# One operand in PSUM for small VectorE instructions of a spectral GNN kernel, and the refinement's products at other units

## The chip, the cores and the metric

The kernel runs on one core of one Trainium2 chip. The metric is the device time of one launch in microseconds (us), from the first to the last instruction with what lies around it; lower is better. TensorE is called PE in the profile, VectorE DVE, ScalarE ACT, GpSimd POOL, SyncE SP.

## What is computed

Two layers on 64 graphs of 256 nodes with 256 features, f32 throughout. Layer 0 is three graph convolutions (256 to 512 to 1024 to 256 features) with the weights `adj * adj`. Layer 1 needs the eigenvectors of a 256 x 256 symmetric matrix made of `adj`, which all graphs share.

```python
# layer 0
h = jnp.maximum(_layernorm(x, axis=-1), 0.0)
h = relu(slconv(h, adj, adj, W1)); h = relu(slconv(h, adj, adj, W2))
x = x + slconv(h, adj, adj, W3)          # slconv: (adj * adj) @ (h @ W)
# layer 1
h = jnp.maximum(_layernorm(x, axis=-1), 0.0)
_, U = jnp.linalg.eigh(L_norm)           # L_norm: scaled Laplacian of adj
agg = jnp.einsum('mn,bnd->bmd', U.T, h)
out = jnp.maximum(agg @ W1 + b1, 0.0) @ W2 + b2
x = x + jnp.einsum('nm,bmd->bnd', U, out)
```

## The kernel before

The graphs go in pairs: 32 pairs, 0 to 31. One pair of layer 0 is a fixed list of 40 units of matmuls on PE (`plan`): 4 `hid` (units 0 to 3), 4 `agg2` (4 to 7), 14 `P` units (8 to 21, two each of P1, P5, P6, P3, P7, P2, P4, seven products in place of eight), 2 `agg` (22, 23, the first product of the next pair), 14 `G` units (24 to 37, another seven products) and 2 `res`. The last pair has no `agg`, so its G units begin at 22. A unit writes one of four PSUM banks in turn; ACT copies each result to SBUF (`evacuate`, L756), POOL forms the sums between products (L556, L564, L572 to L590, all 128 x 512 or 128 x 256 f32 in SBUF), and ACT applies the ReLU to six of them (`finish`, L762). G1 waits for all six (`fin`, L1515).

Beside the pairs runs the eigenvalue problem, mostly one chain on DVE:

- **Householder steps** k = 0 to 253, over pairs 0 to 20. For k up to 126 the vectors span two blocks of 128 (`householder_two`, L945), after that one (`householder_one`). PE lays a column of two numbers per partition out as a row with transposes (L1455): first `col` (`step_x`), then `qcol` (`step_q`). Between these two, and behind the second, PE works off the slice of the pair's units that a table (`GROUPS`: 11 steps per pair in pairs 0 to 7, 12 in 8 to 10, then 13, 12, 14 and 13) gives to the step. DVE scales q by a scalar (L997) before it uses the row of q (L1000), updates A (L963, L967) and makes the next `col` (L1009). POOL keeps each reflector (L503, L504) as soon as v is there (L988), and then does what sums are due.
- **Sturm counts**, four times (`sturm_counts`, L1123): 256 small dependent instructions per direction and, every 16 pivots, a block of start values (L1140) and a block of sign counts (L1167). The first count ends in a product on PE at unit 34 of pair 22 (`COUNTS_AT`).
- **Eigenvectors of the tridiagonal matrix** (L1237 to L1282): two chains of factors, a second pass over all of them (L1249 to L1259), the twist index, two scans each way, a norm whose root ACT takes (L853).
- **Refinement** in pairs 30 and 31: PE turns Z (L1678), then twice Gram and T Z (L1685, L1686), Z^T(TZ) (L1690) and the correction (L1694, L1695), with DVE work between; then the signs, another turn and the products U and U^T (L1699, L1700). `REFINE_AT`, `TURN_AT` and `VECTORS_AT` say before which unit each is placed, counted from unit 0 of pair 30 (40 and more is pair 31).

Layer 1 follows for all pairs (from 2055 us). Engines run their own instruction lists in order, and wait for one another through semaphores only. In `householder_two` every DVE instruction but L997 has at most one tensor operand in SBUF and the other, if any, in PSUM, or is one element wide; L997 reads `qcol` and writes `qn`, both two elements per partition in SBUF.

## Time and profile before

| | us |
|---|---|
| median of 3 runs | 2314.66 |
| range of the runs | 2314.52 to 2315.05 |
| the profiled execution | 2315.77 |
| its span, first to last instruction | 2314.0 |
| Householder steps on two blocks | 19 to 777 |
| Householder steps on one block | 777 to 1380 |
| pairs 21 to 29 beside Sturm counts and factors | 1381 to 1921 |
| pairs 30 and 31 with the refinement | 1921 to 2055 |
| layer 1 | 2055 to 2314 |
| busy: PE, DVE, ACT, POOL | 2259.6, 2005.7, 1149.3, 1172.5 |

The profiled execution lies 1.1 us above the median, and 1.8 us of it lie outside the span. Two engines are busy nearly all the time, so the busy shares alone don't say which one sets the pace; that is read from who waits for whom in each stage.

### The profile page before, as it was taken

Reading aid. Unit: us, or ns where it says so; the run is one execution under the profiler, and the core shown is the slowest. Engines: PE = TensorE matmul, PEld = TensorE weight load, DVE = VectorE, ACT = ScalarE, POOL = GpSimd, SP = SyncE. Lnnn points to the kernel's source line nnn. Section 1 sums busy time; section 2 is a strip of 40 time slices with the busy share of each in tenths; the row PEclk is TensorE's granted clock in tenths of the full one; section 3 lists DMA queues with packets and bytes.
Section 4 is the critical chain, followed back from the end, with each engine's and each line's share of the span. In section 5 each row is a group of like instructions: output and inputs, shape, how many; then the busy total and the mean of one; then the engine's idle time right before and its main releaser. Section 6 shows DMA issues by size and latency. Waiting matters only on the chain.

```text
span 2314.0 us, 47926 instructions
## 1 busy us (share of the span) xinstructions
PE 2259.6 (98%) x12586; PEld 1898.6 (82%) x12586; DVE 2005.7 (87%) x10807; ACT 1149.3 (50%) x2901; POOL 1172.5 (51%) x1889
## 2 busy tenths in 40 slices
PE   7999999999999999999999999999999999999999
PEld 5777777877787788887777788888888888899998
DVE  7999999999999988888888889999999995447776
ACT  5455555555555555554444444454444444345554
POOL 6445554444555555555554567545555554353332
PEclk9999999999999999999999999999999999999999
DMA  3000000000000000000000000000000001024443
GB/s 103 28 28 10 28 28 27 21 28 28 28 10 28 28 29 28 28 28 28 19 28 28 28 29 19 28 19 28 28 28 28 28 28 37 19 67 130 134 133 107
DMA packets 90033, 90.16 MB, mean 39 GB/s; under 512 B 5376, under 2 KB 89088, under 8 KB 89856
## 3 DMA queue, kind: packets, MB, share of 16 engines
q1 hardware_dynamic: 89856, 88.23, 12.0%
q8 instruction: 58, 0.95, 0.2%
q14 instruction: 119, 0.97, 0.1%
HBM read 54.66 MB, written 33.55 MB: 38 GB/s over the span
## 4 chain that ended last, share of the span: by engine, by line
PE 69%; DVE 24%; ACT 4%; issue 2%; POOL 1%; DVEq 0%; POOLq 0%; ACTq 0%
PE ps L1533 53%; PE ps L1723 10%; DVE A L963 3%; DVE qn L997 2%; DVE A L967 2%; PE ps L1455 2%; ACT squares L711 2%; DVE xrow_sb L972 2%; ACT root_s L713 2%; DVE prods L1000 2%; DVE sc L981 1%; DVE ps L1015 1%; PE ps L1733 1%; DVE sc L984 1%; DVE qcol L986 1%
## 5 line engine op out<-in xcount | busy, mean ns | idle before, releaser
L503 POOL COPY Eb<-sc 128x1 f32<-128x1 f32 (+1 forms) x254 | 47.1, 186 | 525.4 <-DVE v L988 292.3
L1533 PE MATMUL ps<-agg2T,w 128*128 128x256 f32 x1024 | 239.8, 379 | 0.0
L1533 PE MATMUL ps<-hid2T,xin 128*128 128x256 f32 x1024 | 236.2, 379 | 1.6 <-ACT h2T L756 1.6
L1533 PE MATMUL ps<-weightT,hid 128*128 128x256 f32 x1024 | 236.6, 380 | 0.0
L1533 PE MATMUL ps<-w,aggT 128*128 128x512 f32 x512 | 231.4, 593 | 0.0
L1533 PEld LDWEIGHTS ps<-weightT,hid 128*128 128x128 f32 x1024 | 189.3, 191 | 35.4 <-issue 13.0
L1533 PEld LDWEIGHTS ps<-hid2T,xin 128*128 128x128 f32 x1024 | 189.5, 190 | 26.3 <-ACT h2T L756 1.9
L1533 PEld LDWEIGHTS ps<-agg2T,w 128*128 128x128 f32 x1024 | 189.2, 191 | 24.2
L756 ACT ACTIVATE hid2T<-ps 128x512 f32<-128x512 f32 x256 | 151.1, 590 | 95.9 <-PE ps L1533 93.2
L1164 DVE SCALAR_TENSOR_TENSOR ahead<-ps,ne,ahead 128x14 f32<-128x14 f32 (+1 forms) x1024 | 190.2, 228 | 0.0
L1161 DVE RECIPROCAL ps<-ahead 128x14 f32<-128x14 f32 (+1 forms) x1024 | 187.8, 229 | 0.1
L1533 PEld LDWEIGHTS ps<-w,aggT 128*128 128x128 f32 x512 | 92.2, 190 | 90.5 <-issue 89.6
L556 POOL TENSOR_TENSOR hid2T<-agg2T 128x512 f32<-128x512 f32 x64 | 82.0, 1281 | 111.7 <-ACT agg2T L756 111.7
L756 ACT ACTIVATE g<-ps 128x128 f32<-128x128 f32 x256 | 70.2, 276 | 136.8 <-PE ps L1533 136.0
L756 ACT ACTIVATE hid<-ps 128x512 f32<-128x512 f32 x128 | 76.3, 596 | 111.4 <-PE ps L1533 110.9
L756 ACT ACTIVATE agg2T<-ps 128x512 f32<-128x512 f32 x128 | 76.2, 595 | 103.5 <-PE ps L1533 103.2
L762 ACT ACTIVATE hid2T<-hid2T 128x512 f32<-128x512 f32 x192 | 119.1, 620 | 9.6 <-POOL hid2T L564 9.3
L1533 PE MATMUL ps<-w3sum,hid 128*128 128x128 f32 x1024 | 123.8, 275 | 0.0
L1533 PE MATMUL ps<-w,hid2T 128*128 128x128 f32 x1024 | 122.9, 275 | 0.0
L1533 PEld LDWEIGHTS ps<-w,hid2T 128*128 128x128 f32 x1024 | 120.7, 192 | 1.3
L713 ACT ACTIVATE root_s<-root_s,tiny 128x1 f32<-128x1 f32 x254 | 74.8, 295 | 93.7 <-DVE prods L1040 88.5
L1455 PE MATMUL ps<-ident,col 128*128 128x128 f32 x381 | 88.3, 286 | 32.5 <-DVE col L1009 30.4
(386 smaller groups left out, 6326.7 us busy)
## 6 DMA issues: line engine op xcount, KB each, us to landing
xl<-in_x_dram SPq DMA_DIRECT2D x64, 256.0 KB, 2.8
xr<-in_x_dram SPq DMA_DIRECT2D x64, 256.0 KB, 2.9
x_dram<-xr SPq DMA_DIRECT2D x64, 256.0 KB, 2.3
xin<-x_dram SPq DMA_DIRECT2D x64, 256.0 KB, 2.8
out_dram<-xin SPq DMA_DIRECT2D x64, 256.0 KB, 2.2
w<-in_L_gnn_W_dram SPq DMA_DIRECT2D x1, 2048.0 KB, 10.3
...
```

Source lines behind the costliest of these rows:

```text
L503: pool.tensor_copy(Eb[:, bass.ds(k, 1)], sc[:, 4:5])
L556: pool.tensor_tensor(moving_sum(n), a, b, ALU.subtract).then_inc(turn_s, 1)
L711: act.activation(squares[:, c0:N], xr[:, c0:N], ACT.Square, accum_out=root_s[:, 0:1]).then_inc(sq, 1)
L713: act.activation(root_s[:, 1:2], root_s[:, 0:1], ACT.Sqrt, bias=tiny[:, 0:1]).then_inc(root, 1)
L756: act.activation(dst, bank, ACT.Relu if stage in ("hid", "P4") else ACT.Copy).then_inc(evac, 1)
L762: act.activation(block_, block_, ACT.Relu).then_inc(fin, 1)
L963: return dve.scalar_tensor_tensor(A[:, b, rest], p_q[:, rest], vh[:, b:b + 1], A[:, b, rest], ALU.mult, ALU.subtract)
L1161: inverse_made[d] = at(dve.reciprocal(inverse[:, d, :], here[:, d, :]))
L1164: pivot_made[d] = at(dve.scalar_tensor_tensor(there[:, d, :], inverse[:, d, :], ne2[:, off:off + 1], there[:, d, :], ALU.mult, ALU.add))
L1455: ins = pe.transpose(dst[:, P * b:P * b + P], col(b).to_broadcast([P, P]), ident[:, 0, 0:P])
L1533: ins = pe.matmul(dst, a, b, start=start, stop=stop, skip_group_check=plan_.units[i][0][0] in "PG")
L1723: ins = pe.matmul(dst, a, b, start=start, stop=stop)
```

## The change

1. L997 becomes a `scalar_tensor_tensor`: q times the scalar, plus two zeros that stand in PSUM (`at_row(p_here, 4)`, set once before the steps).
2. In the Sturm counts the points (`held`), sign counts (`signs`), meeting values and counts move to PSUM, so that each instruction has at most one tensor operand in SBUF. The wait for `gram_saved` moves ahead of the first count, since its banks are used now. One copy per count is added.
3. The second pass over the factors reads the reciprocals where they lie in PSUM; the cap at 1e20 is fused with the multiplication by `ne2` and with that by `pad`; `hot` and `dn` move to PSUM; two whole memsets become two of one column; the squared norm is taken in one instruction per block.
4. In pairs 30 and 31 the refinement's products stand at other units, and ACT takes the root of the norms behind unit 2 of pair 30 instead of unit 7.

```diff
@@ -238,7 +236,8 @@
 
 
         COUNTS_AT, REFLECTORS_AT = 34, 3
-        REFINE_AT, TURN_AT, VECTORS_AT = (10, 13, 19, 23, 28, 34, 41), 60, 62
+        REFINE_AT, TURN_AT, VECTORS_AT = (5, 8, 13, 17, 21, 24, 28), 48, 59
+        NORMS_AT = 2
...
                         ln_apply(pair + 1, 1)
-                    if norms and (stage, j, q) == ("agg2", 1, 1):
+                    if norms and i == NORMS_AT:
                         act.wait_ge(z_root_in, 1)
                         act.activation(nrm[:, 1, :], nrm[:, 0, :], ACT.Sqrt).then_inc(z_root, 1)
...
@@ -994,7 +993,7 @@
                 dve.wait_ge(v_ready, k + 1)
                 at(dve.tensor_scalar(vh, v[:, :], inv_h, None, ALU.mult))
                 dve.wait_ge(q_ready, k + 1)
-                at(dve.tensor_scalar(qn[:, :], qcol[:, :], inv_h, None, ALU.mult))
+                at(dve.scalar_tensor_tensor(qn[:, :], qcol[:, :], inv_h, at_row(p_here, 4), ALU.mult, ALU.add))
...
 
             link(dve.memset(xr[:, :], 0.0))
+            for p_here in p_turn:
+                link(dve.memset(at_row(p_here, 4), 0.0))
...
                 inverse = bank[:, 0:2 * W].rearrange("p (d w) -> p d w", d=2)
-                signs = negs[:, 0:size].rearrange("p (c d w) -> p c d w", c=ROUNDS_OF, d=2)
+                held, total, left, met = (bank[:, 2 * widest + widest * i:2 * widest + widest * i + W] for i in range(4))
+                signs = ps[3][:, 0:size].rearrange("p (c d w) -> p c d w", c=ROUNDS_OF, d=2)
...
@@ -1139,12 +1141,13 @@
                     for d, diag in ((0, Db[:, i:i + n]), (1, Db[:, N - n - i:N - i][:, ::-1])):
                         ins = dve.tensor_tensor(piv[g % 2][:, 0:n, d, :],
                                                 diag.unsqueeze(2).to_broadcast([P, n, W]),
-                                                pts.unsqueeze(1).to_broadcast([P, n, W]), ALU.subtract)
+                                                held.unsqueeze(1).to_broadcast([P, n, W]), ALU.subtract)
...
                 at(dve.memset(signs, 0.0))
+                dve.wait_ge(sturm_v, at(dve.tensor_copy(held, pts)))
...
                     counted = at(dve.scalar_tensor_tensor(signs, piv[g % 2], 0.0, signs, ALU.is_lt, ALU.add))
 
-                down, up_ = piv[TWO_WAY % 2][:, 0, 0, :], piv[(TWO_WAY - 1) % 2][:, ROUNDS_OF - 1, 1, :]
+                down, up_ = left, piv[(TWO_WAY - 1) % 2][:, ROUNDS_OF - 1, 1, :]
...
-            sturm_counts(points0[:, :], C0, ps[1])
-            dve.tensor_copy(cnt0[:, :], cnt[:, 0:C0]).then_inc(cnt_ready, 1)
-
             dve.wait_ge(gram_saved, 1)
+            counts = sturm_counts(points0[:, :], C0, ps[1])
+            dve.tensor_copy(cnt0[:, :], counts).then_inc(cnt_ready, 1)
...
-                link(dve.tensor_reduce(found[:, :], below_j[:, :, :], AX.X, ALU.add))
-                link(dve.scalar_tensor_tensor(lo[:, :], found[:, :], step[:, 0:1], lo[:, :], ALU.mult, ALU.add))
+                in_bracket = ps[2][:, 8 * widest:8 * widest + NB]
+                link(dve.tensor_reduce(in_bracket, below_j[:, :, :], AX.X, ALU.add))
+                link(dve.scalar_tensor_tensor(lo[:, :], in_bracket, step[:, 0:1], lo[:, :], ALU.mult, ALU.add))
...
+
+            def lanes(a, n):
+                return ps[1 + a][:, 0:2 * NB * n].rearrange("p (n c) -> p n c", c=2 * NB)
...
-            RF, QF = Rfb[:, 0:N - 1, :], Qfb[:, 1:N, :]
             for a, n in ((0, P), (1, P - 1)):
-                link(dve.tensor_scalar(Rfb[:, P * a:P * a + n, :].rearrange("p n c -> p (n c)"),
-                                       ps[1 + a][:, 0:2 * NB * n], 1e20, None, ALU.min))
-            for lane, offs, diag in ((chains[0], ne2[:, 0:N - 1], Y[:, :, :]),
-                                     (chains[1], ne2[:, 0:N - 1][:, ::-1], Y[:, ::-1, :])):
-                link(dve.tensor_tensor(QF[:, :, lane], RF[:, :, lane],
-                                       offs.unsqueeze(2).to_broadcast([P, N - 1, NB]), ALU.mult))
-                link(dve.tensor_tensor(QF[:, :, lane], QF[:, :, lane], diag[:, 1:N, :], ALU.add))
-            link(dve.reciprocal(RF, Qfb[:, 0:N - 1, :]))
-            link(dve.tensor_scalar(RF, RF, 1e20, None, ALU.min))
-
-            link(dve.tensor_tensor(gam[:, :, :], Qfb[:, :, 0:NB], Y[:, :, :], ALU.subtract))
-            link(dve.tensor_tensor(gam[:, :, :], gam[:, :, :], Qfb[:, ::-1, NB:2 * NB], ALU.add))
-            link(dve.tensor_tensor(gam[:, :, :], gam[:, :, :], gam[:, :, :], ALU.mult))
-            link(dve.tensor_reduce(gmin[:, :], gam[:, :, :].rearrange("p i a -> p a i"), AX.X, ALU.min))
+                for d, lane in enumerate(chains):
+                    offs = (ne2[:, P * a:P * a + n], ne2[:, 0:N - 1][:, ::-1][:, P * a:P * a + n])[d]
+                    link(dve.scalar_tensor_tensor(lanes(a, n)[:, :, lane], lanes(a, n)[:, :, lane], 1e20,
+                                                  offs.unsqueeze(2).to_broadcast([P, n, NB]), ALU.min, ALU.mult))
+            for a, n in ((0, P), (1, P - 1)):
+                for d, lane in enumerate(chains):
+                    diag = (Y[:, :, :], Y[:, ::-1, :])[d][:, P * a + 1:P * a + 1 + n, :]
+                    link(dve.tensor_tensor(Qfb[:, P * a + 1:P * a + 1 + n, lane], lanes(a, n)[:, :, lane], diag, ALU.add))
+
...
+            for a, n in ((0, P), (1, P - 1)):
+                link(dve.reciprocal(lanes(a, n), Qfb[:, P * a:P * a + n, :]))
+            hot = ps[0][:, :].rearrange("p (b n) -> p b n", b=NB)
+            link(dve.tensor_tensor(hot, gam.rearrange("p n b -> p b n"), gam.rearrange("p n b -> p b n"), ALU.mult))
+            link(dve.tensor_reduce(gmin[:, :], hot, AX.X, ALU.min))
...
-            link(dve.memset(mul_up[:, :, :], 0.0))
-            link(dve.memset(mul_dn[:, :, :], 0.0))
-            for b in range(NB):
-                link(dve.tensor_tensor(mul_up[:, b, 0:N - 1], Rfb[:, 0:N - 1, b], pad[:, 0:N - 1], ALU.mult))
-
-                link(dve.tensor_tensor(mul_dn[:, b, 1:N], Rfb[:, 0:N - 1, NB + b][:, ::-1], pad[:, 0:N - 1], ALU.mult))
+            link(dve.memset(mul_up[:, :, N - 1:N], 0.0))
+            link(dve.memset(mul_dn[:, :, 0:1], 0.0))
+            for a, n in ((0, P), (1, P - 1)):
+                part = lanes(a, n).rearrange("p n c -> p c n")
+                link(dve.scalar_tensor_tensor(mul_up[:, :, P * a:P * a + n], part[:, 0:NB, :], 1e20,
+                                              pad[:, P * a:P * a + n].unsqueeze(1).to_broadcast([P, NB, n]),
+                                              ALU.min, ALU.mult))
+                down_to = slice(N - P * a - n, N - P * a)
+                link(dve.scalar_tensor_tensor(mul_dn[:, :, down_to], part[:, NB:2 * NB, ::-1], 1e20,
+                                              pad[:, N - 1 - P * a - n:N - 1 - P * a].unsqueeze(1).to_broadcast([P, NB, n]),
+                                              ALU.min, ALU.mult))
...
+            link(dve.tensor_tensor(Z[:, :, :], up[:, :, :], dn, ALU.add))
+            link(dve.tensor_tensor(Z[:, :, :], Z[:, :, :], hot, ALU.subtract))
             dve.wait_ge(t_built, 5)
-            link(dve.tensor_tensor(Zsq[:, :, :], Z[:, :, :], Z[:, :, :], ALU.mult))
-            dve.tensor_reduce(nrm[:, 0, :], Zsq[:, :, :], AX.X, ALU.add).then_inc(z_root_in, 1)
+            for b in range(NB):
+                ins = dve.scalar_tensor_tensor(Zsq[:, b, :], Z[:, b, :], 1.0, Z[:, b, :], ALU.mult, ALU.mult,
+                                               accum_out=nrm[:, 0, b:b + 1])
+            ins.then_inc(z_root_in, 1)
```

**VectorE, step 0 of the Householder steps.** Before (L988 is v, L1000 uses the row of q):

```order
L988 SCALAR_TENSOR_TENSOR v<-ident,sc,ps 128x2
L989 TENSOR_SCALAR xrow_sb<-xrow_sb,sc 128x1
L991 RECIPROCAL sc<-sc 128x1
L992 TENSOR_SCALAR ps<-ps,sc 128x1
L995 TENSOR_SCALAR ps<-v,sc 128x2
L997 TENSOR_SCALAR qn<-qcol,sc 128x2
L1000 SCALAR_TENSOR_TENSOR prods,sc<-ps,sc,xrow_sb 128x255
```

After:

```order
L987 SCALAR_TENSOR_TENSOR v<-ident,sc,ps 128x2
L988 TENSOR_SCALAR xrow_sb<-xrow_sb,sc 128x1
L990 RECIPROCAL sc<-sc 128x1
L991 TENSOR_SCALAR ps<-ps,sc 128x1
L994 TENSOR_SCALAR ps<-v,sc 128x2
L996 SCALAR_TENSOR_TENSOR qn<-qcol,sc,ps 128x2
L999 SCALAR_TENSOR_TENSOR prods,sc<-ps,sc,xrow_sb 128x255
```

The order is the same; the one instruction has another form and a PSUM operand (`ps`).

**ScalarE, start of pair 30** (`hid`, `agg2T`, `h2T` are evacuated units, `nrm` is the root of the norms). Before:

```order
L756 ACTIVATE hid<-ps 128x512 x4
L756 ACTIVATE agg2T<-ps 128x512 x4
L853 ACTIVATE nrm<-nrm 128x2
L756 ACTIVATE h2T<-ps 128x512
```

After:

```order
L755 ACTIVATE hid<-ps 128x512 x3
L852 ACTIVATE nrm<-nrm 128x2
L755 ACTIVATE hid<-ps 128x512
L755 ACTIVATE agg2T<-ps 128x512 x4
```

The root moves ahead of five evacuations.

**TensorE, the end of the P units of pair 31.** `hid2T,UT` is P7, `agg2T,w` P2, `hid2T,w` P4, `w,hid2T` G1 and G2; L1678 turns Z, L1666 are the products for U and U^T. Before:

```order
L1533 MATMUL ps<-hid2T,UT 128x256 x4
L1533 MATMUL ps<-agg2T,w 128x256 x8
L1678 MATMUL ps<-ident,Z 128x128 x4
L1533 MATMUL ps<-hid2T,w 128x256 x8
L1666 MATMUL ps<-Zt,QT 128x256 x4
L1666 MATMUL ps<-QT,Zt 128x256 x4
L1701 MATMUL ps<-v,c 128x256
L1702 MATMUL ps<-ident,c 128x128
L1533 MATMUL ps<-w,hid2T 128x128 x16
```

After:

```order
L1551 MATMUL ps<-hid2T,UT 128x256 x4
L1551 MATMUL ps<-agg2T,w 128x256 x4
L1684 MATMUL ps<-Zt,QT 128x256 x4
L1684 MATMUL ps<-QT,Zt 128x256 x4
L1719 MATMUL ps<-v,c 128x256
L1720 MATMUL ps<-ident,c 128x128
L1551 MATMUL ps<-agg2T,w 128x256 x4
L1551 MATMUL ps<-hid2T,w 128x256 x8
L1551 MATMUL ps<-w,hid2T 128x128 x16
```

The products for U no longer stand between P4 and G1, but between the two halves of P2; the turn of Z has moved 12 units ahead.

## Rows read from the trace of the kernel before

**Rows 1.** The page: busy time, and the chain that ended last by engine.

```profile
PE 2259.6 (98%) x12586; PEld 1898.6 (82%) x12586; DVE 2005.7 (87%) x10807; ACT 1149.3 (50%) x2901; POOL 1172.5 (51%) x1889
...
PE 69%; DVE 24%; ACT 4%; issue 2%; POOL 1%; DVEq 0%; POOLq 0%; ACTq 0%
```

**Rows 2.** Waits in 19 to 777 us: who for whom, us, times, longest.

```profile
PE ps L1455 <- DVE col L1009: 30.4, 44, 1.0
...
DVE xrow_sb L972 <- PE ps L1455: 4.6, 4, 3.4
DVE prods L1000 <- PE ps L1455: 1.6, 5, 0.4
```

**Rows 3.** One line's instructions: duration ns min/median/max, first and last start.

```profile
L997 DVE TENSOR_SCALAR qn<-qcol,sc x127: 215/220/1347, 22.1 to 773.2; 128x2 f32<-128x2 f32 x127
...
L1006 DVE SCALAR_TENSOR_TENSOR ps<-ps,sc,qn x127: 216/218/221, 24.3 to 774.2; 128x2 f32<-128x2 f32 x127
```

**Rows 4.** Timeline of 53 to 56 us: start, duration, instruction.

```profile
53.65 1.27 POOL L564 TENSOR_TENSOR hid2T<-spec,hid2T 128x512 f32<-128x512 f32 x1
53.68 1.27 DVE L997 TENSOR_SCALAR qn<-qcol,sc 128x2 f32<-128x2 f32 x1
```

**Rows 5.** L997 by stretches: stretch, its length, busy us (instructions), clock, DMA.

```profile
18.80:90.00 71.20, 8.09 (x11) 1.00 0.04 14
90.00:296.10 206.10, 19.75 (x33) 1.00 0.08 24
296.10:561.20 265.10, 26.45 (x44) 1.00 0.08 25
561.20:692.60 131.40, 8.06 (x24) 1.00 0.08 25
692.60:777.00 84.40, 7.25 (x15) 1.00 0.10 32
```

**Rows 6.** Pair 25, without steps: length, busy PE, PEld, DVE, ACT, POOL.

```profile
1634.15:1691.51 57.36, 57.36 (x306) 48.99 (x304) 56.85 (x337) 27.91 (x66) 30.96 (x34) 1.00 0.08 28
```

**Rows 7.** Timeline of PE at 493 us: a row of q, and what follows.

```profile
493.04 0.38 PE L1455 MATMUL ps<-ident,qcol 128*128 128x128 f32 x2
493.26 2.32 PE L1533 MATMUL ps<-g,weightT 128*128 128x256 f32 x10
```

**Rows 8.** Timeline of DVE: step 126 begins.

```profile
765.35 0.29 DVE L972 COPY xrow_sb<-ps 128x130 f32<-128x130 f32 x1 [0.70 <-PE ps L1455]
```

**Rows 9.** Timeline of pair 30's start: DVE's norms, ACT's third evacuation and its root.

```profile
1925.12 0.69 DVE L1282 TENSOR_REDUCE nrm<-Zsq 128x2 f32<-128x512 f32 x1
1935.87 0.17 DVE L1285 RECIPROCAL nrm<-nrm 128x2 f32<-128x2 f32 x1 [10.05 <-ACT nrm L853]
...
1926.52 0.60 ACT L756 ACTIVATE hid<-ps 128x512 f32<-128x512 f32 x1 [1.12 <-PE ps L1533]
...
1935.64 0.20 ACT L853 ACTIVATE nrm<-nrm 128x2 f32<-128x2 f32 x1
```

**Rows 10.** Timeline of pair 31: the P4 units, the products for U, the last ReLU.

```profile
2031.47 3.62 PE L1533 MATMUL ps<-hid2T,w 128*128 128x256 f32 x16
2034.93 1.89 PE L1666 MATMUL ps<-Zt,QT 128*128 128x256 f32 x8
...
2035.62 0.62 ACT L762 ACTIVATE hid2T<-hid2T 128x512 f32<-128x512 f32 x1
```

**Rows 11.** Timeline behind the second Z^T(TZ): PE's next unit, DVE's last instruction.

```profile
1986.07 1.95 PE L1533 MATMUL ps<-w,agg2T 128*128 128x128 f32 x16
...
1988.51 1.17 DVE L1333 TENSOR_TENSOR below<-tmp,V 128x512 f32<-128x512 f32 x1
```

**Rows 12.** Sturm counts: one line's durations (ns), and DVE's wait at the first count's end.

```profile
L1140 DVE TENSOR_TENSOR ahead<-Db,points x72: 161/384/1511, 1388.7 to 1759.4; 128x224 f32<-128x224 f32 x48, 128x256 f32<-128x256 f32 x16, 128x14 f32<-128x14 f32 x6, 128x16 f32<-128x16 f32 x2
...
DVE tmp L1204 <- PE ps L1598: 2.9, 1, 2.9
```

**Rows 13.** PE's waits in 1380 to 2062 us: the longest (us in total, times, longest).

```profile
PE ps L1533 <- ACT h2T L756: 1.6, 1, 1.6
```

More of the change, by code:

```diff
@@ L135, in gnn_spectral_kernel @@
         gmin = sb("gmin", [P, NB])
-        ahead = sb("ahead", [P, 5 * NB * N])
-        hot, mul_up, mul_dn, up, dn = (ahead[:, NB * N * i:NB * N * (i + 1)].rearrange("p (b n) -> p b n", b=NB)
-                                       for i in range(5))
+        ahead = sb("ahead", [P, 3 * NB * N])
+        mul_up, mul_dn, up = (ahead[:, NB * N * i:NB * N * (i + 1)].rearrange("p (b n) -> p b n", b=NB)
+                              for i in range(3))
         Z = sb("Z", [P, NB, N])
@@ L1164, in sturm_counts @@
                             pivot_made[d] = at(dve.scalar_tensor_tensor(
-                                there[:, d, :], inverse[:, d, :], ne2[:, off:off + 1], there[:, d, :],
+                                left if (i, d) == (P - 1, 0) else there[:, d, :], inverse[:, d, :], ne2[:, off:off + 1], there[:, d, :],
                                 ALU.mult, ALU.add))
                     counted = at(dve.scalar_tensor_tensor(signs, piv[g % 2], 0.0, signs, ALU.is_lt, ALU.add))
-                down, up_ = piv[TWO_WAY % 2][:, 0, 0, :], piv[(TWO_WAY - 1) % 2][:, ROUNDS_OF - 1, 1, :]
+                down, up_ = left, piv[(TWO_WAY - 1) % 2][:, ROUNDS_OF - 1, 1, :]
                 dve.wait_ge(sturm_v, sturm[0])
-                at(dve.tensor_tensor(meet[:, 0, 0:W], down, up_, ALU.add))
+                at(dve.tensor_tensor(met, down, up_, ALU.add))
+                at(dve.tensor_scalar(meet[:, 1, 0:W], held, Db[:, P:P + 1], -1.0, ALU.subtract, ALU.mult))
+                at(dve.tensor_reduce(total, signs.rearrange("p c d w -> p w (c d)"), AX.X, ALU.add))
                 dve.wait_ge(sturm_v, sturm[0])
-                at(dve.tensor_scalar(meet[:, 1, 0:W], pts, Db[:, P:P + 1], -1.0, ALU.subtract, ALU.mult))
-                at(dve.tensor_reduce(cnt[:, 0:W], signs.rearrange("p c d w -> p w (c d)"), AX.X, ALU.add))
+                at(dve.scalar_tensor_tensor(meet[:, 2, 0:W], up_, 0.0, total, ALU.is_lt, ALU.subtract))
+                at(dve.tensor_tensor(met, met, meet[:, 1, 0:W], ALU.is_lt))
                 dve.wait_ge(sturm_v, sturm[0])
-                at(dve.scalar_tensor_tensor(meet[:, 2, 0:W], up_, 0.0, cnt[:, 0:W], ALU.is_lt, ALU.subtract))
-                at(dve.tensor_tensor(meet[:, 1, 0:W], meet[:, 0, 0:W], meet[:, 1, 0:W], ALU.is_lt))
+                at(dve.tensor_tensor(total, met, meet[:, 2, 0:W], ALU.subtract))
                 dve.wait_ge(sturm_v, sturm[0])
-                at(dve.tensor_tensor(cnt[:, 0:W], meet[:, 1, 0:W], meet[:, 2, 0:W], ALU.subtract))
-                dve.wait_ge(sturm_v, sturm[0])
+                return total
             link(dve.tensor_scalar(step[:, :], step[:, :], 1.0 / (P * C0 + 1), None, ALU.mult))
@@ L1216, in _ @@
                                               ALU.mult, ALU.add))
-                sturm_counts(points[:, :, :].rearrange("p a c -> p (a c)"), NB * KS, ps[2])
-                link(dve.tensor_tensor(below_j[:, :, :], cnt[:, 0:NB * KS].rearrange("p (a c) -> p a c", a=NB),
+                counts = sturm_counts(points[:, :, :].rearrange("p a c -> p (a c)"), NB * KS, ps[2])
+                link(dve.tensor_tensor(below_j[:, :, :], counts.rearrange("p (a c) -> p a c", a=NB),
                                        index[:, :].unsqueeze(2).to_broadcast([P, NB, KS]), ALU.is_le))
-                link(dve.tensor_reduce(found[:, :], below_j[:, :, :], AX.X, ALU.add))
-                link(dve.scalar_tensor_tensor(lo[:, :], found[:, :], step[:, 0:1], lo[:, :], ALU.mult, ALU.add))
+                in_bracket = ps[2][:, 8 * widest:8 * widest + NB]
+                link(dve.tensor_reduce(in_bracket, below_j[:, :, :], AX.X, ALU.add))
+                link(dve.scalar_tensor_tensor(lo[:, :], in_bracket, step[:, 0:1], lo[:, :], ALU.mult, ALU.add))
             dve.scalar_tensor_tensor(lam[:, :], step[:, 0:1].to_broadcast([P, NB]), 0.5, lo[:, :],
@@ L1265, in _ @@
+            for a, n in ((0, P), (1, P - 1)):
[3 more added lines that the diff above has]
+            link(dve.tensor_reduce(gmin[:, :], hot, AX.X, ALU.min))
             for b in range(NB):
-                link(dve.tensor_scalar(hot[:, b, :], gam[:, :, b], gmin[:, b:b + 1], None, ALU.is_equal))
+                link(dve.tensor_scalar(hot[:, b, :], hot[:, b, :], gmin[:, b:b + 1], None, ALU.is_equal))
@@ new lines, in _ @@
+            link(dve.memset(mul_dn[:, :, 0:1], 0.0))
+            for a, n in ((0, P), (1, P - 1)):
+                part = lanes(a, n).rearrange("p n c -> p c n")
[6 more added lines that the diff above has]
+                                              ALU.min, ALU.mult))
@@ L1275, in _ @@
+            dn = ps[1][:, :].rearrange("p (b n) -> p b n", b=NB)
             for b in range(NB):
```

7 lines of the change are left out of this document (3 added, 4 removed).

## The prediction, made before the result was known

> **What bounds the kernel now.** I read the page first: PE is busy 98% and carries 69% of the chain that ended last, DVE 24% [rows 1]. From that one would say that DVE doesn't matter. The waits by stage say otherwise. In 19 to 777 us, the Householder steps on two blocks, PE waits 30.4 us for `col`, 44 times, while DVE waits for PE 6.2 us, of which 3.4 are the very first step [rows 2]. There DVE is the bound, and what is taken out of its chain comes out of the time, as long as PE can follow. From 1381 us on it is the reverse: pair 25 takes 57.36 us and PE is busy for all of them [rows 6], and up to 2062 us PE's longest wait is 1.6 us, once [rows 13]. There an earlier DVE gives nothing, and a later one costs only once it is so late that PE or ACT has to stop.
>
> **L997, q scaled.** Its median is 220 ns, its maximum 1347 [rows 3]. The timeline shows the long form: POOL starts a 128x512 addition at 53.65, L997 starts at 53.68 and lasts 1.27 us, to just behind POOL's end [rows 4]. POOL has just been released by v, as it is in each step, so the two meet wherever a sum is due. L1006 has the same shape and the form that L997 will get (one tensor in SBUF, one in PSUM); it runs 127 times through the same stage, also beside POOL's additions, and never takes more than 221 ns [rows 3].
> The Trainium skill (SBUF — State Buffer, "Who interferes with whom") says why: GpSimd and VectorE share a pair of SBUF ports as an exclusive lock, a `tensor_scalar` can take it, and an instruction with at most one SBUF input outside the 2-port modes does not. By that rule L997's stall goes altogether, and the trace agrees (221 ns at most). The Trainium skill also speaks against moving operands (VectorE: DVE Perf Modes, "Why PSUM operands drop a tier"): f32 with a PSUM operand is held to one element per cycle. With two elements that is no price here, 218 against 220 ns.
> So L997 falls to 0.22 us. What goes is busy time less 0.22 us each [rows 5]: 8.09 - 2.42 = 5.7; 19.75 - 7.26 = 12.5; 26.45 - 9.68 = 16.8; 8.06 - 5.28 = 2.8; 7.25 - 3.30 = 4.0; in all 41.7 us.
>
> **How much of it PE lets through.** PE's own work per pair is 57.36 us [rows 6] plus the rows of the steps: two transposes hold it for 493.26 - 493.04 = 0.22 us [rows 7], so 0.44 per step, 4.8 for 11 steps and 5.2 for 12. The floors: pair 0, 62.2 us of 71.2; pairs 1 to 3, 186.5 of 206.1; pairs 4 to 7, 248.6 of 265.1; pairs 8 and 9, 125.2 of 131.4; pair 10 with three steps of pair 11, about 77 of 84.4 [rows 5, 6]. Room is there for 9.0, 19.6, 16.5, 6.2 and 7 us, so only in pairs 4 to 7 is the stall (16.8) a little larger than the room: 41.4 us by stretches.
> Within a stretch the steps are uneven, since a matmul can't be cut and the pauses fall into some steps only. I therefore walked the 126 steps one by one: DVE's four pieces per step with their own durations, PE's slice at 216 ns per 256-column matmul, 112 per 128 and 429 per 512, a row at 0.22 (0.27 if PE had to wait). For the kernel before, the walk starts step 126 at 763.9 us, where the trace has 765.3 [rows 8]. With L997 at 220 ns everywhere it ends 38.0 us earlier; the 3.7 that are lost are DVE's waits for a row that PE is late with. I take 38.0. The stall vanishing only in part, or ACT's root coming late since its evacuations stand closer together, would make it less; I put the lower end at 28. The steps on one block don't change. PE and DVE both come out of the stage earlier, and everything behind it moves as a block, because the pairs' slices are tied to the steps. The two memsets of the zeros stand once in front of step 0: 0.1 to 0.2 us each, 0.3 us on the path.
>
> **Sturm counts and factors.** L1140 has a median of 384 ns and a maximum of 1511 [rows 12], the same meeting with POOL, now with two SBUF inputs; the other moved lines likewise. I estimate 10 to 20 us less for the three later counts and the fused pass together (54 blocks like L1140 in three counts, a part of them up to 1.1 us long over). What the first count gains is lost at once, DVE already waits 2.9 us there for PE's unit 34 [rows 12]. None of it shows in the time: PE is the bound [rows 6]. Its cover if it went the other way is small though. DVE finishes the norms at 1925.8; ACT will take their root behind its third evacuation, at about 1927.0 [rows 9]. A chain that is 1.2 us later makes ACT stop, in order, with the evacuations behind it, and then PE. The added copy (four times some 0.2 us) and the earlier `gram_saved` wait (long over by the first count) are far inside the gain. POOL meets DVE less while it sets up pair 21, which may take up to 1.6 us from PE's one wait [rows 13]; I count 0.
>
> **Refinement at other units.** The same 7 products, the same PE work; only waits can change.
> - Turn of Z: today the root comes at 1935.64 and DVE waits 10.05 us for it [rows 9]. Both ACT's root and PE's turn move by five units, 8.6 us. The two POOL additions that overlap DVE's scaling of Z today don't lie there then; 0.3 us gain.
> - Second correction, now 4 G units (4 x 0.89 = 3.6 us) behind Z^T(TZ), before 7 units. DVE needs from 1986.07 to 1988.51 + 1.17 = 1989.7, or 3.6 us [rows 11], 3.1 without the stretch in L1333. Just enough; 0 to 1 us, I take 0.2. The other gaps keep 3 us and more.
> - G1 of pair 31: before, the products for U (4 us) stand between the last P4 unit and G1. P4 ends at 2034.93 and the ReLU that G1 waits for at 2035.62 + 0.62 = 2036.24 [rows 10], 1.3 us later. In other pairs two `agg` units cover that, the last pair has none. With the products gone from there PE waits 1.3 us, plus 0.15 to start: a loss of 1.5 us that the profile of before doesn't show, since its cover was there.
>
> The Trainium skill's lock rule would also bear on the second item: the corrections' three instructions with two SBUF inputs may each be held by an addition of POOL. If POOL's run of additions reached 2 us further, that would be up to 2 us more.
>
> **The sum**, against the profiled execution: 2315.8 - 38.0 + 0.3 - 0.3 + 0.2 + 1.5 = 2279.5. That execution lies 1.1 us above the median of 2314.7, so the median is forecast at 2278.3 us, rounded to 2278.
>
> **Rivals.**
> - A: the gain is smaller, because PE or ACT is late more often than in the walk (ACT's squares queue behind evacuations, PE's uneven slices): 28 to 33 us instead of 38, time 2283 to 2288. For it: the room in pairs 4 to 9 is small, 3 to 4 us per pair. Against: the walk, which has these waits in it, repeats the stage before within 1.4 us. Chance 13%.
> - B: the full 41.7 us and PE's 1.6 us at pair 21: about 2272. Chance 8%.
> - C: the form doesn't free L997, which waits for POOL as before (so the change doesn't do what it says for this line): no gain, 2315 to 2317 with the 1.5 us at G1. Against: L1006. Chance 4%.
> - D, slower than before: PSUM operands make the moved instructions slower and the Sturm and factor chain later. About 120 instructions are moved. From 1.2 us net (the slack above) it costs PE as much as it is late. To eat the whole gain the chain must lose 1.2 + 38 us beyond the 15 or so that the meetings give back, which is 0.45 us per instruction; at 0.6 us each it is 120 x 0.6 - 15 - 1.2 = 56 us late, and the time 2278 + 56 = 2334. L1006, with its PSUM operand at 218 ns, speaks against it. Chance 2%.
> - My forecast, 2275 to 2282: 73%.
>
> **Range.** 80% and a little more: from 2273 (towards B) to 2288 (A whole). A measurement of this kernel tells 0.2%, or 4.6 us, from no change. Faster by more than that: 94%. Within it (C): 4%. Slower (D): 2%.
>
> **What would show it.** In the profile of after: L996 with a maximum near 220 ns and about 28 us busy instead of 69.6; PE's wait for `col` down from 30.4 us to well under 10, and DVE's waits for rows up from 6 to about 10; the step on two blocks ending near 739 us; pairs of 57.4 us from then on, unchanged; a new wait of about 1.4 us of PE for ACT's ReLU at G1 of pair 31; DVE waiting longer for the root. I'm wrong if L996 keeps long forms (C), if ACT's root or DVE's waits for rows grow by more than 10 us (A), or if PE waits for Z (D).

## The result, and the profile after

The changed kernel takes **2277.99 us** (median of 4 runs, 2277.96 to 2278.76), the kernel before in the same comparison 2314.86 (4 runs, 2314.52 to 2315.75). The ratio is 0.9841 with a 95% interval of 0.9824 to 0.9858: faster by 36.9 us, or 1.6%. The forecast was 2278, range 2273 to 2288.

The profiled execution took 2277.98 us with a span of 2276.3 us. Its page (busy time; chain that ended last, by engine), against [rows 1]:

```profile
PE 2250.6 (99%) x12586; PEld 1898.8 (83%) x12586; DVE 1929.3 (85%) x10818; ACT 1149.3 (50%) x2901; POOL 1159.4 (51%) x1889
...
PE 87%; DVE 10%; ACT 2%; issue 1%; POOL 0%; DMA 0%; SPq 0%; DVEq 0%; POOLq 0%; ACTq 0%
```

PE does the same 12586 matmuls. DVE's share of the chain fell from 24% to 10%. DVE's busy time fell by 76 us, twice the gain. 43 of them are L997's; the other 33, which the Sturm and factor parts saved, hardly show in the time.

The scaling of q (L996 now) and its neighbour of like shape, in the stage on two blocks (duration ns min/median/max, first and last start), against [rows 3], then the line's total (busy us, mean ns, idle before):

```profile
L996 DVE SCALAR_TENSOR_TENSOR qn<-qcol,sc,ps x127: 205/207/217, 21.3 to 733.8; 128x2 f32<-128x2 f32 x127
...
L1005 DVE SCALAR_TENSOR_TENSOR ps<-ps,sc,qn x127: 217/218/221, 23.0 to 734.8; 128x2 f32<-128x2 f32 x127
```

```profile
L996 DVE SCALAR_TENSOR_TENSOR qn<-qcol,sc,ps 128x2 f32<-128x2 f32 x127 | 26.3, 207 | 0.0
```

The maximum went from 1347 ns to 217, the busy time from 69.6 us to 26.3. The waits of that stage (18 to 739 us, so that the wait for the very first row is in, as it is in [rows 2]; who for whom, us, times, longest):

```profile
DVE sc L978 <- ACT root_s L712: 11.9, 62, 0.2
...
DVE xrow_sb L971 <- PE ps L1473: 3.9, 8, 2.1
...
DVE prods L999 <- PE ps L1473: 2.8, 9, 0.5
...
PE ps L1473 <- DVE col L1008: 0.6, 3, 0.2
```

PE's wait for `col` fell from 30.4 us to 0.6. It didn't vanish ahead of PE as a whole: the weight load of that row, which stands in front of the matmul, waited 60.5 us for `col` before and still waits 21.6 us.

```profile
PEld ps L1455 <- DVE col L1009: 60.5, 80, 1.6
```

```profile
PEld ps L1473 <- DVE col L1008: 21.6, 53, 1.1
```

The step whose start [rows 8] have at 765.35 (its row is 130 wide and that of k = 0 is 255, so it is k = 125, the 126th; "step 126" here and below) begins at

```profile
725.96 0.29 DVE L971 COPY xrow_sb<-ps 128x130 f32<-128x130 f32 x1 [0.47 <-PE ps L1473]
```

39.4 us earlier, and 38.6 us earlier if both are counted from the start of k = 0. From pair 11 on each pair starts 38.7 to 39.8 us earlier than before, up to pair 30 (1921.17 us before, 1881.40 after). Pair 25 (stretch, its length, busy PE, PEld, DVE, ACT, POOL) is the 57.36 us of [rows 6]:

```profile
1594.38:1651.74 57.36, 57.36 (x305) 48.99 (x304) 56.85 (x372) 27.89 (x66) 30.08 (x34) 1.00 0.08 28
```

In the last two pairs some of it goes back. The waits of the whole run that matter from pair 21 on:

```profile
DVE nrm L1303 <- ACT nrm L852: 31.5, 1, 31.5
...
PE ps L1551 <- ACT hid2T L761: 1.3, 1, 1.3
...
PE ps L1551 <- ACT h2T L755: 0.7, 1, 0.7
...
PE ps L1684 <- DVE below L1351: 0.5, 1, 0.5
```

The first is DVE, early with the norms and waiting for their root (10.05 us before, [rows 9]). The second is G1 of pair 31, the wait that was foretold; the third is the wait of [rows 13], in pair 21, 1.6 us before; the fourth stands ahead of the second correction.

### The profile page after: what moved, and what is told of

Read it like the earlier page. It is cut to its first block, busy times and chain, and to the rows that moved or that the text cites. A ratio compares the mean times of both kernels' runs of the same rounds, so it can differ in the third digit from the quotient of the medians.

```text
span 2276.3 us, 47938 instructions
## 1 busy us (share of the span) xinstructions
PE 2250.6 (99%) x12586; PEld 1898.8 (83%) x12586; DVE 1929.3 (85%) x10818; ACT 1149.3 (50%) x2901; POOL 1159.4 (51%) x1889
## 4 chain that ended last, share of the span: by engine, by line
PE 87%; DVE 10%; ACT 2%; issue 1%; POOL 0%; DMA 0%; SPq 0%; DVEq 0%; POOLq 0%; ACTq 0%
PE ps L1551 70%; PE ps L1741 10%; PE ps L1473 4%; DVE A L962 1%; PE ps L1751 1%; PE ps L1684 1%; DVE A L966 1%; ACT root_s L712 1%; ACT squares L710 1%; DVE prods L999 1%; DVE xrow_sb L971 1%; DVE ps L1014 0%; DVE sc L980 0%; DVE sc L983 0%; DVE qcol L985 0%
## 5 line engine op out<-in xcount | busy, mean ns | idle before, releaser
L1551 PE MATMUL ps<-hid2T,w 128*128 128x256 f32 x512 | 120.1, 379 | 0.0
```

Of the source, the lines that this page charges most:

```text
L1551: ins = pe.matmul(dst, a, b, start=start, stop=stop, skip_group_check=plan_.units[i][0][0] in "PG")
```

## How the runs are compared

Each run's ratio is against the kernel before on the same chip. From trace to trace PE's first matmul of pair 0 starts somewhere between 17.8 and 19.3 us, also where nothing ahead of it differs (18.0 in after, 19.0 in e4): as much as some of the differences looked for. The last column therefore counts from that matmul to the end of the span; "the count" below is this column. It comes from one trace per kernel. Where the code is the same the traces repeat closely: pair 25 takes 57.36 us in all twelve, and from the first matmul to pair 30, which is the same in after, e4 and e9, they take 1863.4, 1863.1 and 1863.1 us. So 0.3 us in this column says nothing, and 0.6 us is little.

| kernel | median us | ratio (95%) | span | first matmul | from there to the end |
|---|---|---|---|---|---|
| before | 2314.9 | 1 | 2314.0 | 18.8 | 2295.2 |
| after | 2278.0 | 0.9841 (0.9824-0.9858) | 2276.3 | 18.0 | 2258.2 |
| e1 part 1 alone | 2277.6 | 0.9835 (0.9820-0.9850) | 2276.0 | 19.2 | 2256.8 |
| e2 all but part 1 | 2316.4 | 1.0005 (0.9996-1.0014) | 2315.1 | 19.1 | 2296.0 |
| e3 parts 1 and 4 | 2278.3 | 0.9840 (0.9825-0.9855) | 2276.9 | 18.1 | 2258.8 |
| e4 two entries of part 4 later | 2276.3 | 0.9830 (0.9817-0.9844) | 2274.6 | 19.0 | 2255.6 |
| e5 zero in SBUF | 2316.6 | 1.0006 (0.9996-1.0016) | 2313.8 | 18.1 | 2295.7 |
| e6 two single elements | 2286.9 | 0.9878 (0.9861-0.9894) | 2286.2 | 19.1 | 2267.2 |
| e7 steps spread anew | 2275.5 | 0.9829 (0.9813-0.9846) | 2273.5 | 17.8 | 2255.8 |
| e8 GpSimd a copy later | 2287.0 | 0.9881 (0.9864-0.9897) | 2284.8 | 18.4 | 2266.5 |
| e9 all but part 4 | 2276.8 | 0.9835 (0.9819-0.9852) | 2274.7 | 18.8 | 2255.9 |
| e10 three steps moved | 2273.4 | 0.9819 (0.9802-0.9835) | 2272.1 | 19.3 | 2252.8 |

## Which part brings the time: e1, e2, e3 and e9

**e1** is the kernel before with this alone:

```diff
-  at(dve.tensor_scalar(qn[:, :], qcol[:, :], inv_h, None, ALU.mult))
+  at(dve.scalar_tensor_tensor(qn[:, :], qcol[:, :], inv_h, at_row(p_here, 4), ALU.mult, ALU.add))
...
+  for p_here in p_turn:
+      link(dve.memset(at_row(p_here, 4), 0.0))
```

> The kernel before with part 1 alone: L997 becomes the three-operand form that adds a zero held in PSUM (and the two memsets for the zeros). My theory: the whole gain sits here, and parts 2 to 4 gave nothing back; without part 4 the 1.3 us that PE waits for the ReLU of pair 31 and the 0.5 us before the second correction are not spent, so the time is 2276.0 us, between 2275 and 2277. Rival: the Sturm and factor parts bring part of the 36.9 us; then this one ends at 2280 us or more, up to 2300 if they bring half.

2277.6 us, 0.6 above the range that was given; by the count it is 2256.8, 38.4 less than before. PE's first matmul comes 1.2 us later in this trace than in that of after, and the expectation had left such a difference out. The mechanism stands: one instruction of 127 executions carries the gain.

**e2** is the changed kernel with the first diff line turned back.

> The changed kernel with q scaled in SBUF again, as before, all else as changed. My theory: the 36.9 us come back, and the waits of part 4 stay: 2315 to 2317 us, with the scaling of q again some 546 ns in the mean where another engine's work runs beside it. Rival (parts 2 to 4 bring part of the gain): 2300 to 2313 us.

2316.4 us, as forecast. By the count it is 37.8 us more than after, and its line (busy us, mean ns) is that of before again:

```profile
L996 DVE TENSOR_SCALAR qn<-qcol,sc 128x2 f32<-128x2 f32 x127 | 69.3, 546 | 0.0
```

**e3** has parts 1 and 4, with the Sturm counts, the factors and the norms in the text of before.

> The changed kernel with the Sturm counts, the factors and the norms written as before (parts 1 and 4 alone). My theory: what the new form saves VectorE, some 20 us by the wait for the root of the norms, which grew from 10.05 to 31.5 us, lies under TensorE; the wait falls to about 10 us and the time stays 2278.0 us, within 0.5. Rival: TensorE's turn of Z, now at unit 5 of pair 30, needs the earlier norms; then it waits, and the time rises by up to the shift of the chain less the room, some 5 to 10 us, to 2283 to 2288.

2278.3 us, as forecast. DVE's wait for the root did not fall to 10 us, as expected, but to 1.4:

```profile
DVE nrm L1288 <- ACT nrm L854: 1.4, 1, 1.4
```

So the new form makes DVE's chain up to the norms 31.5 - 1.4 = 30.1 us shorter, more than the 10 to 20 that were estimated, and 0.6 us of it show in the count. What is left with the old text is a thin cover: the norms end at 1886.66 us and ACT starts their root at 1887.86, so by this trace a chain more than 1.2 us longer would have made ACT stop. This was not run.

**e9** is the changed kernel with part 4 turned back:

```diff
-  REFINE_AT, TURN_AT, VECTORS_AT = (5, 8, 13, 17, 21, 24, 28), 48, 59
-  NORMS_AT = 2
+  REFINE_AT, TURN_AT, VECTORS_AT = (10, 13, 19, 23, 28, 34, 41), 60, 62
...
-  if norms and i == NORMS_AT:
+  if norms and (stage, j, q) == ("agg2", 1, 1):
```

> The changed kernel without part 4 alone: refinement, turns of Z, eigenvectors and norms at the units of before. Counted from TensorE's first unit of pair 0 to the end of the span (which leaves out the start, different by up to 1.4 us from trace to trace), the runs so far give 2295.2 us before, 2256.8 with part 1 alone, 2258.8 with parts 1 and 4, 2258.2 with all. My theory: part 4 costs 2.0 us and the Sturm and factor forms give 0.6: 2256.2 us by this count, 2276 to 2277 in time. Rival: part 4 costs nothing by itself, and is needed for what the Sturm part gives: 2258 us by this count.

2255.9 by the count, 2276.8 us. The six kernels together give each part twice: part 1 38.4 us less alone (before to e1) and 37.8 on top of the others (e2 to after); the Sturm and factor forms 0.6 less with part 4 (e3 to after) and 0.9 less without it (e1 to e9); part 4 2.0 us **more** with the old Sturm text (e1 to e3) and 2.3 more with the new one (e9 to after). Two stretches say the same with less noise: pair 21 takes 0.8 us less with the new Sturm text, and from pair 30 to the end part 4 costs 2.0 us with either.

## What part 4 costs, and how much of it can be had back: e4

```diff
-  REFINE_AT, TURN_AT, VECTORS_AT = (5, 8, 13, 17, 21, 24, 28), 48, 59
+  REFINE_AT, TURN_AT, VECTORS_AT = (5, 8, 13, 17, 21, 24, 29), 48, 62
```

> The changed kernel with two numbers of part 4 changed: the last correction stands ahead of unit 29 instead of 28, and the eigenvectors' products ahead of unit 62 instead of 59. My theory: the 1.3 us that TensorE waits at G1 of pair 31 for the ReLU, and nothing else, hang on the second number: the products come at the place they had before, the wait falls to 0 and the time to 2276.7 us (2276.2 if the 0.2 us by which the first correction of the last moves matters too). Rival: the wait only moves to the next G unit or to the end, where the eigenvectors are then late: 2278 us or more.

2276.3 us, as forecast, and 2.6 less than after by the count. Both waits are gone. In after they look like this; first G1 of pair 31 (timeline of ACT and PE: start, duration, instruction, the idle time before it and its releaser):

```profile
2000.33 0.62 ACT L761 ACTIVATE hid2T<-hid2T 128x512 f32<-128x512 f32 x1
...
2001.06 1.86 PEld L1551 LDWEIGHTS ps<-w,hid2T 128*128 128x128 f32 x16 [1.67 <-ACT hid2T L755]
2001.09 1.91 PE L1551 MATMUL ps<-w,hid2T 128*128 128x128 f32 x15 [1.30 <-ACT hid2T L761]
```

then the second correction:

```profile
1937.02 2.95 POOL L582 TENSOR_TENSOR agg2T<-hid2T,hid 128x512 f32<-128x512 f32 x2
...
1938.88 1.65 DVE L1350 SCALAR_TENSOR_TENSOR tmp<-prods,tmp 128x512 f32<-128x512 f32 x1
...
1940.56 0.69 DVE L1351 TENSOR_TENSOR below<-tmp,V 128x512 f32<-128x512 f32 x1
...
1941.31 0.92 PE L1684 MATMUL ps<-below,Z 128*128 128x256 f32 x3 [0.52 <-DVE below L1351]
```

L1350 has both tensor inputs in SBUF. It begins while POOL's two additions run (up to 1939.97) and lasts 1.65 us. The same instruction in the trace of before, L1332, had no POOL beside it but for its last 0.07 us, and took 0.69; there the long one was the next, L1333, 1.17 us [rows 11].

```profile
1987.78 0.69 DVE L1332 SCALAR_TENSOR_TENSOR tmp<-prods,tmp 128x512 f32<-128x512 f32 x1
```

The meeting moved by an instruction and grew from 0.5 to 1.0 us, and PE waited 0.5 us for it. In e4 the meeting is the same, and L1350 takes 1.64 us. What is different is that PE has one unit more to do ahead of the correction, so `below` is there in time:

```profile
1937.70 2.94 POOL L582 TENSOR_TENSOR agg2T<-hid2T,hid 128x512 f32<-128x512 f32 x2
...
1939.55 1.64 DVE L1350 SCALAR_TENSOR_TENSOR tmp<-prods,tmp 128x512 f32<-128x512 f32 x1
...
1941.30 1.06 PE L1551 MATMUL ps<-w3sum,hid 128*128 128x128 f32 x8
...
1942.19 1.89 PE L1684 MATMUL ps<-below,Z 128*128 128x256 f32 x8
```

So e4 doesn't take the hold away, it covers it.

## Why the new operand helps: e5, e6 and e8

**e5** keeps the three-operand instruction and moves its zero into SBUF:

```diff
-  at(dve.scalar_tensor_tensor(qn[:, :], qcol[:, :], inv_h, at_row(p_here, 4), ALU.mult, ALU.add))
+  at(dve.scalar_tensor_tensor(qn[:, :], qcol[:, :], inv_h, zq[:, :], ALU.mult, ALU.add))
```

> The changed kernel with one operand moved: the zero that is added to the scaled q lies in SBUF, so the same three-operand instruction has both tensor operands in SBUF. Theory 1 (what VectorE waits for is its grip on the port that it shares with GpSimd, which an instruction with two SBUF operands wants too): the instruction is stretched as in the kernel before, by some 330 ns in the mean, and the time is 2314 to 2318 us. Theory 2 (only the two-operand form, which may run in a faster mode, waits; the three-operand form does not, wherever its operands lie): some 207 ns each and 2278 us.

Theory 1, in full: 2316.6 us. By line and in the timeline:

```profile
L997 DVE SCALAR_TENSOR_TENSOR qn<-qcol,sc,zq 128x2 f32<-128x2 f32 x127 | 67.2, 529 | 0.0
```

```profile
52.91 1.27 POOL L564 TENSOR_TENSOR hid2T<-spec,hid2T 128x512 f32<-128x512 f32 x1
52.94 1.26 DVE L997 SCALAR_TENSOR_TENSOR qn<-qcol,sc,zq 128x2 f32<-128x2 f32 x1
```

So the three-operand form by itself frees nothing: in it, where the second tensor input lies decides (the first input and the output lie in SBUF both times). Of the 127 scalings of e2, 42 begin while a long instruction of POOL (over 0.5 us) has more than 0.1 us left, and 41 of them are held; of the 77 that begin with none near, none is held. In after 44 begin so and none is held. One more comparison stands in the trace of before: L995 is the two-operand form on two elements too, but writes to PSUM, and it never takes more than 226 ns, though 10 of its 127 begin beside a running addition. That q's scaling would be free as well if only its output lay in PSUM was not run. The Trainium skill (SBUF — State Buffer, "Who interferes with whom") names both cases: the two-port modes of a `tensor_scalar`, and two SBUF inputs against a GpSimd instruction that reads SBUF. This case has one of each, e2 and e5, at nearly the same price (546 and 529 ns in the mean).

**e6** scales q in SBUF in the old form, one element at a time:

```diff
-  at(dve.scalar_tensor_tensor(qn[:, :], qcol[:, :], inv_h, at_row(p_here, 4), ALU.mult, ALU.add))
+  for b in range(NB):
+      ins = dve.tensor_scalar(qn[:, b:b + 1], qcol[:, b:b + 1], inv_h, None, ALU.mult)
+  at(ins)
```

> The changed kernel with q scaled in SBUF by the old two-operand form, but one element per partition at a time: two instructions in place of one. In the kernel before, instructions of this form on one element (L980, L983) are not stretched. My theory: neither are these; the second one adds some 210 ns in each of 126 two-block steps, 26.5 us, of which some 3 us lie in room that TensorE leaves: 2300 to 2303 us, with no instruction of this line over 300 ns. Rival (every scaling that lies wholly in SBUF waits at this place, whatever its length): 2330 us or more, with single ones of 800 ns and longer.

```profile
L997 DVE TENSOR_SCALAR qn<-qcol,sc x254: 201/204/215, 22.3 to 744.3; 128x1 f32<-128x1 f32 x127
```

Not one of 254 is held, as expected: the same operation, wholly in SBUF, beside the same additions. The time was missed by 13 us (2286.9 against 2300 to 2303). The timeline shows the error:

```profile
53.31 0.22 DVE L994 TENSOR_SCALAR ps<-v,sc 128x2 f32<-128x2 f32 x1
53.41 1.27 POOL L563 TENSOR_TENSOR hid2T<-spec,hid2T 128x512 f32<-128x512 f32 x1
53.44 0.33 DVE L997 TENSOR_SCALAR qn<-qcol,sc 128x1 f32<-128x1 f32 x2
...
53.68 0.47 DVE L1001 SCALAR_TENSOR_TENSOR prods<-ps,sc,xrow_sb 128x250 f32<-128x250 f32 x1
```

An addition has begun 0.03 us ahead, as in [rows 4], and both instructions together take 0.33 us, not 0.41. Over the 127 steps the second starts 122 ns behind the first in the mean, so it adds 127 x 0.122 = 15.5 us to DVE's chain and not 26.5. Step 126 starts 9.2 us later than in after, counted from step 0; the rest lay in room.

**e8** goes at the other side: it is e2, with q scaled as before, and GpSimd makes one copy more in each step.

```diff
  pool.tensor_copy(V[:, b0:NB, bass.ds(k, 1)].squeeze(2), v[:, b0:NB]).then_inc(v_saved, 1)
+ pool.tensor_copy(idle[:, bass.ds(k, 1)], ones[:, 0:1])
```

> As e2 (the changed kernel with q scaled in SBUF again), and in each step GpSimd makes one more copy of one column, of a constant to a place that nobody reads, behind the copy of v. The extra copy takes some 184 ns by its neighbours (L502, L503). In the traces of before and of e2 the stretched scalings of q are those ahead of which, by 28 to 40 ns, a tensor_tensor of GpSimd has begun; the copy of v is what holds that tensor_tensor to this moment in each step. My theory: with the extra copy GpSimd's instruction begins some 150 ns behind the start of the scaling, VectorE has the port first, and at most 8 of the 127 instructions are over 300 ns: 2278 to 2284 us, though nothing on VectorE or TensorE is changed against e2 (2316). Rival 1: VectorE is held as well by one that begins during its instruction: the stretched ones stay some 40 and the time 2313 us or more. Rival 2: what is stretched is due to the form and TensorE's reads of q, and GpSimd's time is chance: unchanged.

```profile
52.93 0.18 POOL L505 COPY idle<-ones 128x1 f32<-128x1 f32 x1
52.98 0.22 DVE L998 TENSOR_SCALAR qn<-qcol,sc 128x2 f32<-128x2 f32 x1
53.06 1.27 POOL L565 TENSOR_TENSOR hid2T<-spec,hid2T 128x512 f32<-128x512 f32 x1
```

POOL's addition now begins 0.08 us behind the scaling instead of 0.03 ahead of it, and the scaling takes 0.22 us. In e2 and in the kernel before 43 of 127 are over 300 ns and 36 over 1000; here 18 and 3, and the mean falls from 546 to 296 ns:

```profile
L998 DVE TENSOR_SCALAR qn<-qcol,sc 128x2 f32<-128x2 f32 x127 | 37.6, 296 | 0.0
```

With nothing changed on DVE or PE against e2 this gives back 29 of the 38 us. At 2287.0 us the time is 3 us above the range that was given (2278 to 2284), and 18 are long instead of at most 8. Rival 2 falls, and Rival 1 as a rule. The reason for the 18 is in the trace too:

```profile
64.04 1.27 POOL L577 TENSOR_TENSOR hid<-hid,hid2T 128x512 f32<-128x512 f32 x1
...
64.96 0.38 DVE L998 TENSOR_SCALAR qn<-qcol,sc 128x2 f32<-128x2 f32 x1
```

There an addition that began 0.92 us earlier is still running when the scaling comes, and the scaling ends 22 ns behind it. Eleven of the 18 are meetings with this addition (L577), once in each pair: the extra copy moved POOL's work against DVE's, and with it the meetings. Some exceptions are left open. In one step of e8 the addition began 43 ns behind the scaling, and the scaling took 1332 ns all the same. In e2 there are two, with additions 49 and 103 ns behind (1344 and 866 ns), while six others with 55 to 58 ns behind were not held.

## Can DVE's room be used: e7 and e10

e7 spreads the 254 steps anew, with e4's units.

```diff
-  GROUPS = [(n, n + 1, 11, 0.54) for n in range(8)]
-  GROUPS += [(8, 10, 12, 0.54), (10, 11, 12, 0.54), (11, 12, 13, 0.54), (12, 16, 12, 0.54), (16, 20, 14, 0.54),
-             (20, 21, 13, 0.54)]
+  GROUPS = [(n, n + 1, 10, 0.54) for n in range(3)]
+  GROUPS += [(n, n + 1, 11, 0.54) for n in range(3, 9)]
+  GROUPS += [(9, 11, 12, 0.54), (11, 12, 12, 0.54)]
+  GROUPS += [(n, n + 1, 13, 0.54) for n in range(12, 16)]
+  GROUPS += [(16, 20, 14, 0.54), (20, 21, 14, 0.54)]
```

> The changed kernel with the later units of the run before, and with the 254 steps spread anew over the 21 pairs: 10 steps in pairs 0 to 2, 11 in pairs 3 to 8, 12 in 9 to 11, 13 in 12 to 15, 14 in 16 to 20 (now 11 in 0 to 7, 12 in 8 to 11 but 13 in 11, 12 in 12 to 15, 14 in 16 to 19, 13 in 20). In the trace of the changed kernel a pair with two-block steps takes 62.5 to 66.1 us by VectorE's steps against 62.2 by TensorE's matmuls, and a pair of the one-block stage is held by TensorE at 60.2 us with room on VectorE. My theory: with the steps where VectorE has room, the larger of the two sums over the pairs falls from 1311 to 1300 us: 2266 us, between 2264 and 2270. Rival: VectorE's steps take longer in pairs whose other work on it is the same, or the room is used already by the lead one engine has over the other from pair to pair: within 2 us of 2277.

2275.5 us: the forecast of 2266 missed by 9, and the rival came true. It gained nothing: 2255.8 by the count, where e4 has 2255.6 (the 0.8 us between the medians lie within the difference of the starts). Pairs 0, 1, 2, 8 and 11, each with a step less, became 2.5, 1.5, 0.8, 2.1 and 2.3 us shorter, 9.2 in all; pairs 12 to 15 and 20, each with a step more, took back 8.5. Stretches of pairs 12 to 15, e7's first, then e4's (length, busy PE, PEld, DVE, ACT, POOL), and PE's weight loads waiting in each:

```profile
775.52:1023.84 248.32, 246.65 (x1322) 200.23 (x1321) 218.25 (x1300) 124.30 (x316) 134.15 (x237) 1.00 0.08 27
```

```profile
PEld ps L1475 <- DVE qcol L1054: 12.3, 25, 1.3
...
PEld ps L1475 <- DVE col L1076: 5.1, 20, 0.5
```

```profile
784.96:1025.82 240.86, 240.85 (x1314) 202.17 (x1313) 200.87 (x1202) 122.64 (x312) 132.93 (x229) 1.00 0.08 27
```

```profile
PEld ps L1473 <- DVE qcol L1052: 2.9, 8, 0.4
```

The four pairs are 7.46 us longer. A step more makes a pair 7.46 / 4 = 1.9 us longer there, and not by the 0.2 us that PE needs for its rows: q and `col` come late for the weight loads. The sum that the expectation rested on took the larger of two sums for each pair, as if DVE's room could be filled without a gap. DVE's steps and PE's units take turns here, and waits for each other cost time before either engine is full. That this is why e7 missed is read from these waits, not tested apart.

**e10** uses the prices that e7's trace shows, and moves three steps only: pairs 0, 8 and 11 give one each, pairs 14, 15 and 20 take one.

```diff
+  GROUPS = [(0, 1, 10, 0.54)] + [(n, n + 1, 11, 0.54) for n in range(1, 9)]
+  GROUPS += [(9, 11, 12, 0.54), (11, 12, 12, 0.54), (12, 14, 12, 0.54), (14, 15, 13, 0.54), (15, 16, 13, 0.54),
+             (16, 20, 14, 0.54), (20, 21, 14, 0.54)]
```

> The changed kernel with the later units of e4, and three steps moved where e7 paid for each by the lengths of the pairs in its trace: pair 0 has 10 steps (2.5 us shorter there), pair 8 has 11 (2.1), pair 11 has 12 (2.3), and pairs 14, 15 and 20 have one more (1.6, 1.6 and 1.1 us longer). My theory: 6.9 - 4.3 = 2.6 us less than e4: 2253.0 us from TensorE's first unit to the end (e4 2255.6), some 2273.7 us in time. Rival: a pair's length hangs on the steps ahead of it (VectorE's lead), and the sum stays as it stayed in e7: 2255.6 and 2276.3 us.

2273.4 us, and 2252.8 by the count, 2.8 less than e4 where 2.6 was forecast. It is the fastest kernel measured here: 4.6 us under the changed kernel by the medians, 5.4 by the count.

## Why the prediction was right, step by step

Terms of its sum, with what the runs showed:

| step | predicted | measured |
|---|---|---|
| L997 at its normal duration, through the stage | -38.0 | -38.4 (before to e1); step 126 against step 0: -38.6 |
| memsets of the zeros | +0.3 | inside the -38.4 |
| Sturm and factor forms | 0 | -0.6 and -0.9 |
| part 4, three terms | +1.4 | +2.0 and +2.3 |
| sum by the count | -36.3 | -37.0 |

- **That DVE bounds the stage on two blocks** held, though PE was busy 96% there too (725.4 of 758.0 us). The test was the pair of waits [rows 2], and they turned over as said.
- **That L997 is held by POOL, and that one PSUM operand frees it**: shown from three sides: e2 and e5 (held), e6 (one element at a time, not held), e8 (POOL moved).
- **How much PE lets through.** The bare stall was 41.7 us, and the walk through the steps said 38.0. This step carried the precision: without it the forecast would have been 3.7 us lower. The walk itself is not among the runs, so it can be held only against its result. If its "step 126" was k = 126 and not the k = 125 of [rows 8], its match with the stage before was off by 6.6 us (that step starts at 770.5) and not by 1.4. The result, 38.0 against 38.6 measured, was right; where the 3.7 us go was right only in part. The walk put them all into DVE's waits for rows, which were to rise from 6 to about 10 us. They went from 6.2 to 6.7. Without the very first row (3.4 us before, 2.1 after) they rose from 2.8 to 4.6. From start to start of DVE's instructions, from k = 0 to step 126, L997 gives 41.4 us. Of these 2.0 go into longer idle times, 1.4 ahead of L999 and 0.6 ahead of L971, and 0.9 into other DVE instructions that became a little longer (L999 0.4, L1001 behind it 0.3): what is left are the 38.6 measured. Why those became longer stays open.
- **The two memsets** were put on the path with 0.3 us. In the trace they lie under DVE's first wait for a row (3.36 us before, 2.05 after); they cost nothing that can be seen.
- **The Sturm part at nothing** was right within a microsecond: 30.1 us shorter on DVE, at most 0.9 in the time. That remainder is in pair 21, 59.17 us before and in e3, 58.33 in after, where PE's wait for `h2T` fell from 1.6 to 0.7 us. The prediction had named it (POOL meets DVE less there) and counted 0 of up to 1.6. The 10 to 20 us that it gave for DVE's saving were too low.
- **The second correction**, 0 to 1 us with 0.2 taken, is the term that was sized too small. PE waits 0.5 us for it in the trace, and from pair 30's start to the end e4 takes 392.5 us, after 394.9: 2.3 us, of which G1 has 1.3 and its start some 0.15, which leaves 0.8 or so for the correction. Pair 30, which holds the correction and not G1, says the same: 75.85 us after, 75.07 in e4. The step had reckoned with a stretch like that of L1333, 0.5 us; the one that came was 1.0 (L1350, 1.65 us against 0.69 alone). The prediction's own sentence on the lock, that each of the three instructions may be held there, fits this trace.
- **The turn of Z, 0.3 us gained**: the same stretch takes 392.9 us with the old units (before, e1 and e9) and 392.5 in e4. It fits, and the wait that goes is one of the weight load, 0.5 us in before and in e9 and none in e4:

```profile
PEld ps L1678 <- DVE Z L1287: 0.5, 1, 0.5
```

- **G1 of pair 31, 1.5 us**: a wait of 1.3 us at the place and for the releaser named.

Rival A (late roots or evacuations) did not come: DVE's waits for ACT's root are 11.9 us, 12.1 before. Rival C fell with L996's maximum of 217 ns, and D with the 30.1 us. By the count the terms of part 1 were 0.7 us better than forecast, the Sturm part 0.6 to 0.9 better and part 4 0.6 to 0.9 worse: 0.7 in all. That the median, 2278.0, lies 0.3 from the unrounded 2278.3 is luck in part.
